# A two-layer graph network on one core: overflow-row counts moved from VectorE to GpSimd, bias parts split there too, and the order of a quad redrawn

## What is computed

```python
def layer0(x, adj, W1, b1, W2, b2):
    mask = (adj > 0.0)
    xj = x @ W1[:F]                                    # F = 64, H = 192
    diff = x[:, :, None, :] - x[:, None, :, :]
    h = relu(xj[:, :, None, :] + diff @ W1[F:] + b1)   # 128 x 128 pairs per graph
    hm = einsum('bjkh,bjk->bjh', h, mask)
    return hm @ W2 + deg[..., None] * b2
x = layernorm(x + layer0(x, adj, ...))
m = relu(relu(x @ W1g + b1g) @ W2g + b2g);  msg = relu(adj @ m)
r, z, n = gates(msg @ W_ih.T + b_ih, x @ W_hh.T + b_hh)
out = layernorm(x + (1 - z) * n + z * x)
```

## Time and profile before

| | us |
|---|---|
| median of 3 runs | 948.43 (948.24 to 950.02) |
| the profiled execution, time of its own | 949.64 |
| its span, first to last instruction | 947.9 |
| PE busy | 856.4 (90%) |
| DVE busy | 841.1 (89%) |
| ACT busy | 563.1 (59%) |
| POOL busy | 309.3 (33%) |

### The profile page before, as it was taken

One profiled execution on the slowest core, in us unless ns is written; L12 is line 12 of the kernel. 1 busy time (PEld: TensorE's weight loads), 2 busy tenths in 40 slices (PEclk: granted clock), 3 DMA queues, 4 the chain that ended last, 5 costly groups with the idle time before them and its releaser, 6 DMA issues.

```text
span 947.9 us, 24988 instructions
## 1 busy us (share of the span) xinstructions
PE 856.4 (90%) x10132; PEld 598.1 (63%) x10132; DVE 841.1 (89%) x1055; ACT 563.1 (59%) x1627; POOL 309.3 (33%) x300
## 2 busy tenths in 40 slices
PE   2678889999999999999999999999999999999983
PEld 1345556767666666767666666777666666667652
DVE  5479999999999999999999999999999999998742
ACT  3433435666676656667675757667675757656442
POOL 2111111242423424242423424242433424242451
PEclk9769999999999999999999999999999999999987
DMA  4122121322113221322113121321213122221000
GB/s 137 27 47 79 46 79 29 80 46 67 41 46 90 47 73 47 80 58 50 58 46 91 46 71 49 79 58 37 72 46 91 45 64 57 46 54 33 1 12 24
DMA packets 31426, 53.27 MB, mean 56 GB/s; under 512 B 8138, under 2 KB 16973, under 8 KB 31309
## 3 DMA queue, kind: packets, MB, share of 16 engines
q1 hardware_dynamic: 31308, 51.65, 21.2%
HBM read 13.87 MB, written 4.19 MB: 19 GB/s over the span
## 4 chain that ended last, share of the span: by engine, by line
PE 64%; DVE 18%; issue 11%; SPq 2%; ACT 2%; DMA 0%; POOL 0%; POOLq 0%; DVEq 0%
PE PS L772 16%; PE PS L781 11%; DVE AC L1094 8%; DVE AC L1083 5%; PE PS L625 3%; PE PS L758 3%; PE PS L838 3%; PE PS L855 2%; PE PS L646 2%; PE PS L826 2%; PE PS L764 2%; PE PS L601 2%; PE PS L612 2%; PE PS L849 2%; PE PS L570 1%
## 5 line engine op out<-in xcount | busy, mean ns | idle before, releaser
L1094 DVE SCALAR_TENSOR_TENSOR AC<-PS,AC 128x1152 f32<-128x1152 f32 (+1 forms) x288 | 351.1, 1219 | 43.0 <-PE PS L772 41.3
L1083 DVE SCALAR_TENSOR_TENSOR AC<-PS,AC 128x1152 f32<-128x1152 f32 (+1 forms) x288 | 350.8, 1218 | 22.6 <-PE PS L781 22.5
L772 PE MATMUL PS<-DM,VA 128*128 128x192 fp8e5 (+1 forms) x1152 | 135.6, 241 | 17.1 <-DVE AC L1083 13.7
L772 PE MATMUL PS<-DM,VB 128*128 128x192 fp8e5 (+1 forms) x1152 | 136.1, 241 | 0.0
L781 PE MATMUL PS<-DM,VB 128*64 128x192 fp8e5 (+1 forms) x1152 | 95.8, 245 | 32.7 <-DVE AC L1094 31.5
L772 PEld LDWEIGHTS PS<-DM,VA 128*128 128x128 f16 x1152 | 89.0, 100 | 44.3 <-DVE AC L1083 28.6
L781 PEld LDWEIGHTS PS<-DM,VB 128*64 128x64 f16 x1152 | 46.7, 109 | 91.2 <-issue 53.3
L772 PEld LDWEIGHTS PS<-DM,VB 128*128 128x128 f16 x1152 | 75.9, 98 | 37.1 <-issue 0.9
L781 PE MATMUL PS<-DM,VA 128*64 128x192 fp8e5 (+1 forms) x1152 | 98.9, 252 | 0.0
L1530 POOL MEMSET AC<- 128x768 f32 x32 | 24.0, 749 | 221.0 <-DVE DM L1064 145.0
L1537 POOL TENSOR_TENSOR AC<-AC,NNB 128x512 f32<-128x512 f32 x64 | 66.0, 1051 | 62.1 <-DVE DM L1061 39.6
(11 more groups left out here) (221 smaller groups left out, 1850.1 us busy)
## 6 DMA issues: line engine op xcount, KB each, us to landing
CW<-WM SPq DMA_DIRECT2D x128, 160.0 KB, 2.8
AT<-in_adjt SPq DMA_DIRECT2D x16, 512.0 KB, 4.0
VA<-VN SPq DMA_DIRECT2D x64, 96.0 KB, 2.2
VB<-VN SPq DMA_DIRECT2D x64, 96.0 KB, 2.2
XN<-in_xn SPq DMA_DIRECT2D x16, 256.0 KB, 4.0
out<-YO SPq DMA_DIRECT2D x15, 256.0 KB, 2.2
cs<-in_cst SPq DMA_DIRECT2D x1, 550.5 KB, 3.6
out<-YO SPq DMA_DIRECT2D x2, 128.0 KB, 1.7
```

The lines of the kernel that those rows point to most:

```text
L772: last = e.matmul(PS[:, b + i % 2, 256 * (i // 2) + cols.start:256 * (i // 2) + cols.stop], lhs[:, GRAPH[i], 0:128], d[:, i, :], start=Fal ...
L1083: e.scalar_tensor_tensor(dst, tiles(PS[:, b:b + 3, :])[:, :, cols], 0.0, dst, ALU.max, ALU.add).then_inc(s["sx"], 1)
L1094: e.scalar_tensor_tensor(dst, tiles(PS[:, b:b + 3, :])[:, :, cols], 0.0, dst, ALU.max, ALU.add).then_inc(s["sy"], 1)
```

## The change

`count(g)` runs on GpSimd. The ten thresholds and their sum are gone; instead the count comes out of a scaled value by adding and taking away 12582912.0, which rounds it to a whole number, and a maximum with 0. That is nine instructions, each waiting for the one before over a semaphore. ACT copies the running sums from PSUM into `VE` (a new ACT instruction at `off`), and DVE's `SI` compare reads `VE` in SBUF instead of PSUM. DVE's copy to `VE` is gone.

The bias vectors are loaded on all 128 partitions by the first two weight DMAs, `parts()` splits them into three bf16 parts on GpSimd (seven instructions, ahead of `split_x(0)` and `count(0)` in its order), and DVE copies one row of each part into `br` and `br2`. `fold()` on DVE is divided: `wide_w()` (nine instructions and six small copies) before the first quad is prepared, and the rest after its `words`. In `prep(0)` the `x_turn`s come before the table steps, and the two `v`s take both banks.

```diff
 ORDER = (
-    ("s2", "p3pde", "te", "ep", "", "t", "", "dprtp", "r", "t", "repee4", "", "d", "pe", "rpd", "e", "p", "wpr0e", "c1"),
-    ("sd2p", "pp3", "", "t", "d", "etpp", "", "l4tcpt", "n", "dp", "d", "np", "d", "d", "w0ddrp", "", "pd", "dp", "1e"),
+    ("2s", "3p", "et", "pep", "", "dtd", "r", "t", "er", "t", "preeep", "pe", "r4d", "p", "p", "ed", "", "crp0", "wep1"),
+    ("sdp2", "pp3", "", "t", "d", "ptpl", "", "4ptt", "c", "denp", "dn", "p", "d", "d", "w0drdp", "e", "pd", "pd", "1"),
 )
...
             do("consts")
+            do("parts")
             finish(ranks(0))
+            do("wide_w")
...
-            for _ in range(4):
+            for _ in range(6):
                 next(link["p"])
             do("fold")
...
             def off(g, b, gates):
                 io = iot[:].unsqueeze(1).to_broadcast([128, 2 * GB, 64])
-                ve.wait_ge(s["off"], g + 1)
+                ve.wait_ge(s["ve"], g + 1)
...
-                                PS[:, b, 0:2 * GB].unsqueeze(2).to_broadcast([128, 2 * GB, 64]), ALU.is_ge)
-                e.tensor_copy(VE[:, g * GB:(g + 1) * GB, :].rearrange("p b k -> p (b k)"),
-                              PS[:, b, 0:2 * GB]).then_inc(s["ss"], 1)
+                                VE[:, g * GB:(g + 1) * GB, :].rearrange("p b k -> p (b k)").unsqueeze(2).to_broadcast([128, 2 * GB, 64]),
+                                ALU.is_ge).then_inc(s["ss"], 1)
...
+            def off(g, b, gates):
+                ac.wait_ge(s["off"], g + 1)
+                e.activation(VE[:, g * GB:(g + 1) * GB, :].rearrange("p b k -> p (b k)"), PS[:, b, 0:2 * GB],
+                             ACT.Copy).then_inc(s["ve"], 1)
...
+            def parts():
+
+                po.wait_ge(s["db"], 32)
+                e.tensor_scalar(be[:, 0:H], bs[:, 0:H], -0.5 * SCALE, None, ALU.mult)
+                e.tensor_copy(be[:, H:H + F], bs[:, H:H + F]).then_inc(s["bb"], 1)
+                for k in range(3):
+                    po.wait_ge(s["bb"], 2 * k + 1)
+                    e.tensor_copy(bp[:, k, :], be[:]).then_inc(s["bb"], 1)
+                    if k < 2:
+                        po.wait_ge(s["bb"], 2 * k + 2)
+                        e.tensor_tensor(be[:], be[:], bp[:, k, :], ALU.subtract).then_inc(s["bb"], 1)
...
+                po.wait_ge(s["ct"], 4 * g + 3)
+                e.tensor_scalar(CT[:], CT[:], WHOLE, None, ALU.add).then_inc(s["ct"], 1)
+                po.wait_ge(s["ct"], 4 * g + 4)
+                e.tensor_scalar(CM[:], CT[:], -WHOLE, None, ALU.add).then_inc(s["cm"], 1)
+                po.wait_ge(s["cm"], g + 1)
+                po.wait_ge(s["off"], g)
+                e.tensor_scalar(NV[:], CM[:], 0.0, None, ALU.max).then_inc(s["nv"], 1)
```

More of the change, by code:

```diff
@@ L165, in follow @@
     order(do)
-DW = 14
+DW = 7
 GRAPH = (0, 2, 1, 3)
@@ L410, in ranks, with table @@
                 do("off", g, *here)
-                bank.give(here[0], "ss", g + 1)
-            def prep(q):
-                yield from bank.spare()
-                here = bank.take()
-                do("ov", q, *here)
-                bank.give(here[0], "ov", q + 1)
-                yield
+                bank.give(here[0], "ve", g + 1)
+            def table(q):
                 yield from bank.spare()
@@ L436, in prep @@
                     yield
-                for k in range(2):
-                    yield from bank.spare()
-                    here = bank.take()
-                    do("v", q, k, *here)
+            def prep(q):
+                yield from bank.spare()
+                here = bank.take()
+                do("ov", q, *here)
+                bank.give(here[0], "ov", q + 1)
+                yield
+                if q:
+                    yield from table(q)
+                    yield from turns(q)
+                    for k in range(2):
+                        yield from bank.spare()
+                        here = bank.take()
+                        do("v", q, k, *here)
+                        yield
+                        do("v_low", q, k, *here)
+                        bank.give(here[0], "vl", 2 * q + k + 1)
+                        yield
+                else:
+                    yield from turns(q)
+                    yield from table(q)
+                    yield from bank.spare(2)
+                    both = bank.take(), bank.take()
+                    for k in range(2):
+                        do("v", q, k, *both[k])
                     yield
-                    do("v_low", q, k, *here)
-                    bank.give(here[0], "vl", 2 * q + k + 1)
+                    for k in range(2):
+                        do("v_low", q, k, *both[k])
+                        bank.give(both[k][0], "vl", 2 * q + k + 1)
                     yield
@@ L1180, in fsum @@
                 e.tensor_copy(fi[:], PS[0:1, b, 0:1]).then_inc(s["flag"], 1)
[L1182 removed]
+            follow(main_order, {"consts": consts, "mask": mask, "off": off, "words": words,
                                 "dgen": dgen, "switch": switch, "round_a": round_a, "round_b": round_b,
[L1184 removed]
+                                "wide_w": wide_w, "fold": fold, "bias": bias, "flag": flag, "fsum": fsum,
                                 **vector_layer1(e, ve, s)})
@@ L1541, in dgen @@
                 po.wait_ge(s["dd"], RD * t + m + 1)
-            follow(main_order, {"setup": setup, "split_x": split_x, "split_xg": split_xg, "clear": clear, "seeds": seeds, "dgen": dgen, **gpsimd_layer1(e, po, s)})
+            follow(main_order, {"setup": setup, "parts": parts, "count": count, "split_x": split_x, "split_xg": split_xg, "clear": clear, "seeds": seeds, "dgen": dgen, **gpsimd_layer1(e, po, s)})
         def gpsimd_dense(e):
```

154 lines of the change are left out of this document (70 added, 84 removed), and 4 rows, old and new, of the table MAIN.

## The result

The changed kernel took 939.7 us (median of 5 runs, 938.57 to 943.15), the kernel before 948.92 beside it (948.24 to 950.45). The ratio is 0.9904, 95% interval 0.9882 to 0.9926: faster by 1.0%, where 2.3% was forecast. The profiled execution lasted 939.27 us with a span of 935.7.

A forecast was written before the change was run, and what follows sets the result against it. PE and DVE hand the bound to each other in the count's half; PE bounds the other. 949.64 - 16.8 (pairs) - 4.6 (start) = 928.2 us, 927.0 against the median; range 921.4 to 932.3.

The forecast's parts named there:

- the steady pair: Two successive quads: PE loses 1.27 us of waits for DVE, gain 1.2 us a pair, 14 times, 16.8 us.
- (a): Count on GpSimd stays hidden: six hops take 1.7 us, NV comes 5 us before PE's need, 2.5 us of count fit.
- Rival 3: GpSimd late with NV, so PE waits at off: 976.5 us if a hop costs 1.65 us; chance 0.05.
- (c): Feature DMAs behind ACT's second v_low (v_out): slack shrinks from 1.4 to 0.2 us, taken as just fitting.
- Rival 1: v_out holds the next quad: PE waits 0.7 us for VA, pair gains 0.5, 936.8 us; chance 0.16.
- the start: Before quad 1: 7.8 us saved, ov 3.2 us later, so v_out 4.6 us earlier; bounds 2.5 and 6.
- about 6 us by the burst at the start: Start: time when the bias is loaded and GpSimd begins the parts, which end near 10 us.
- quads 1 to 5: Early quads with two counts: forecast change -2.4 us.
- nothing at the ends: Tail, with its old tables, and time outside the span: forecast change 0.
- The range: Forecast's own range: 921.4 us (14 x 1.5 + 6) to 932.3 us (14 x 0.9 + 3.5).
- hangs on SP: Quad 0: layer 1's 30 DMAs queue behind v_out, bias waits for the last, so 4.6 us arrive at quad 1.
- Rival 2: DVE and GpSimd block at SBUF: 942.4 us if words are held (chance 0.08), 966.2 with SI too (0.05).

The follow-up runs named there:

- e1: Changed kernel with the count back on DVE (the seven instructions of before), copy to VE still on ACT: 961.24 us.
- e6: Changed kernel with XHL's subtraction made twice on GpSimd, the first into a tile that nobody reads: 948.66 us.
- e2: Changed kernel with the two old ORDER strings; count on GpSimd, VE on ACT and the new start stay: 945.34 us.
- e4: Changed kernel with ACT's second v_low put ahead of layer 1's four scalings: 937.52 us.
- e12: Changed kernel run again without an edit: 937.63 us.
- e11: Changed kernel with the seven bias-part instructions back on DVE, the count staying on GpSimd: 932.58 us.
- e7: Changed kernel with bias parts behind the first count on GpSimd and ACT's second v_low ahead of the four scalings: 934.49 us.
- e9: Changed kernel with 21 of layer 1's 30 weight DMAs in quad 0, 9 in quad 1, and its bias in quad 2: 940.02 us.
- e3: Changed kernel with the bias parts moved behind the first split_x and count on GpSimd: 936.61 us.
- e8: Changed kernel with all 30 of layer 1's weight DMAs in quad 1 and its bias in quad 2: 946.85 us.
- e13: Changed kernel with bias parts on DVE and ACT's second v_low ahead of the four scalings: 931.77 us.
- e14: Changed kernel with bias parts on DVE, plus a memset and one unused f32-to-bf16 copy on GpSimd at the start: 934.21 us.

## Why the prediction was wrong

**Right in number, in part by luck: the steady pair.** "I take 1.2 us a pair" came out as 1.11. DVE goes from round to round, the 1.02 us wait is gone, and e1 prices the count at the 1.49 that the profile of before shows. But the sum was that "1.02 + 0.25 = 1.27 us of waits" go and that "PE is the bound to the end of the half", and that isn't what happened. The waits for DVE ahead of a `round_b` fell by 8.7 us in twelve pairs, 0.7 a pair. One of 0.30 us now stands at 526.42 and one of 0.53 at 512.79, where there was one of 0.26. The other 0.4 us of the 1.11 isn't in a wait that the trace shows, and I can't place it.

**Right: the cover of the count, (a).** The hops are 0.29 to 0.35 us, and the first, held by the words, is 0.84; the six take 2.4 us, and `NV` is there 4.3 us ahead of PE's use. "2.5 us of count fit" left 1.1 us at XGl (e6), but only in the new order (e2), which puts the count ahead of XGl. Rival 3 needed a hop of 1.36 us.

**Wrong: (c), "just fitting".** The slack of 1.4 - 1.2 = 0.2 us came out as 0.3, but I worked it out with a landing of 2.2 us, which is a median. In the changed kernel the landings of `VB` reach 3.5 us. In the trace of before they do too (up to 3.7), but the slack took up all but one. Rival 1 had the right place, and a price for every pair; it came in five or six of fourteen, 3.2 us of waits in the table's third row (e4 takes them away, at 0.14 us a half).

What the late transfers have in common is on the page's DMA queues: beside the kernel's own transfers a queue named "instruction" moves packets, of 8 or 16 KB in this stretch. From 100 us on, the sixteen traces have 264 transfers to `VA` and `VB` that landed more than 2.5 us after issue, and during every one of them such a packet was moving. Without one, none of 1258 took more than 2.25 us; with one, 334 still landed in time. The wait of 0.77 us above, from the issue to PE's start (packets, MB, share of 16 engines):

```profile
q8 instruction: 1, 0.02, 2.4%
```

No run moved these packets, so that they are the cause is not shown.

**Wrong: the start.** From `ov`'s first matmul on the path is 9.85 us where it was 17.4: 7.6 us saved, and 7.8 was forecast. The failed term is "about 6 us by the burst at the start" for the landing of the bias, which no row supported: it was 8.08, and 9.17 in e12. The load is issued behind those of x and the adjacency and lands after that of x in both runs (6.48 and 8.64). The seven instructions took 3.8 us, inside my 3.5 to 5, `ov` came at 16.87 instead of 14.8, and `v_out` 2.35 us earlier instead of 4.6, below my lower bound of 2.5. Of that, 1.6 arrive at quad 1. The larger mistake is not in a term. I never asked whether the parts had to leave DVE: it stands idle for 9.31 us ahead of `SI` and 3.53 ahead of the words. e11 puts them there, where they cost nothing.

**Chance: quads 1 to 5.** They gained 1.3 us where 2.4 were forecast, and in e12 the same program gained 3.3. Quad 2 alone differs by 1.75 us, by the clock.

**Wrong: nothing at the ends.** The tail with its old instructions lasts 1.2 us longer. It goes with the granted clock. Four matmuls of the chain show it (before, then after), and so do the tails as a whole (before, after, e7; the columns as in the earlier trace rows):

```profile
927.37 1.13 PE PS L568 x4
...
914.29 2.07 PE PS L586 x4
...
861.63:947.90 86.27, 65.33 (x633) 46.02 (x630) 48.18 (x81) 36.26 (x126) 30.25 (x31) 0.89 0.06 18
...
848.18:935.70 87.52, 66.38 (x631) 46.97 (x630) 48.02 (x81) 35.90 (x125) 29.00 (x29) 0.87 0.06 18
...
843.68:929.60 85.92, 65.16 (x633) 45.90 (x630) 48.01 (x81) 36.42 (x127) 28.98 (x29) 0.89 0.06 18
```

e7 and e9 have the changed kernel's tail at the mean clock of before, 0.89, and theirs lasts 86.0 us in both, 0.3 less than before; at 0.85 (e3) it lasts 88.7. One run fits less well, e8 with 88.4 at 0.87. The time outside the span grew by 1.9 us. All 70 executions of kernels with the parts on GpSimd have 2.4 to 4.3 us there; those without (before, e11, e13, e14) have 1.6 to 2.1. That the parts go with it is shown, why they do is open; e14 excludes one type-changing copy by itself.

**The range.** The slow end of the forecast's own range, 932.3 us, takes 0.9 us a pair and 3.5 for the start, though the bounds named beside the terms were 0.6 and 2.5. With those it would be 937.5, still below the measured 939.7.

**Half wrong: quad 0 "hangs on SP".** It does (e8, e9: 2.4 us), but what stands behind it doesn't let the gain through: the words in e8, the bias between rounds in e9.

**Rival 2** exists and costs nearly nothing here. The prediction had the overlap missed "by a few hundredths" and priced it at 1.1 us. It is there in every steady half with a count, and the words take 0.92 us instead of 0.82 in it (up to 0.99 elsewhere); the count's first instruction takes 0.76 instead of 0.30. Neither is on the path for more than a tenth. `SI` with two inputs in SBUF stayed at 1.21 to 1.23 us. The Trainium skill (SBUF — State Buffer, "SBUF: two separate sides") lets the first comer keep the shared port pair for its whole instruction. The rows of e6 agree in both directions, 0.58 us for the subtraction that comes second, 0.10 for the words. They don't show the hold to the end: the subtraction had 0.24 us of its recorded time left when the words began.
